# Layer-0 attention of a two-layer graph kernel: masked scores kept in PSUM, the softmax division given to GpSimd, and the steps of a turn in another order

## The chip, the cores and the metric

The kernel runs on one core of a Trainium2 chip. The metric is the device time of one execution in microseconds (us), the median of several.

## The reference

There are 64 independent graphs of 128 nodes with 256 features, and an adjacency matrix `adj` of zeros and ones for each. Two layers follow one another.

```python
# layer 0: 8 heads of 32, masked softmax, MLP of 1024
nx = LN(x) ; q, k, v = nx@wq+bq, nx@wk+bk, nx@wv+bv
scores = q@k.T / sqrt(32) + where(adj > 0, 0.1*adj*adj, -inf)
out = softmax(scores) @ v
x1 = x + out@wo + bo
x2 = x1 + gelu(LN(x1)@w1 + b1)@w2 + b2
# layer 1: one head of 256
w = softmax(where(adj == 0, -inf, (x2@Wq)@(x2@Wk).T / 16))
y = LN(x2 + (w @ (x2@Wv))@Wo + bo1) * gamma + beta
```

## The kernel before, in words

Each engine has its program written out by hand, and semaphores tie the five programs together. Work goes by groups: 4 graphs, 512 tokens, except for the first and the last group with 2 graphs each, which makes 17 groups. One turn of the kernel's loop works on four groups at once: `gp` (layer norm, queries, keys, values, scores and probabilities), `ga`, the group before it (attention output, `x1`, second layer norm), `gb`, the one before that (MLP and most of layer 1), and `gc` (the closing layer norm and the store). The turns for gp = 3 to 15 are alike (gp = 4 to 15 are a loop of 12); the turn of gp = 16 has half a group, and `first_turn` and `last_turn` are written apart. Every matrix product of the big layers is three TensorE matmuls (`mm3`, L395 to L400), of the high and low parts of both operands, so most copies out of PSUM come as a pair: ScalarE writes the high part, VectorE the low part (`low`, L1184). A wait for a low part is a wait for both.

The probabilities of layer 0 are worked on in pairs of graphs, q = 0 and 1, and within a pair in four parts r = 0 to 3, one PSUM bank each (banks 0 to 3). A part goes this way:

- `scores(gp, q)` on TensorE (L559) fills banks 0 to 3.
- `biased(g, q, r)` on VectorE (L1292, four instructions of 128x128, each with a read of the accumulator) subtracts the scores from the mask and writes the result to the SBUF tile `p_s`, with the row's extreme in `neg_max`.
- `exps` on ScalarE (L950, four of 128x128, each with an accumulator read) reads `p_s` and writes the exponentials back to the PSUM bank, sums in `psum`.
- `divided` on VectorE: the reciprocal of the sums (L1300), and a 128x512 multiplication out of the bank into `p_s` (L1302).
- `blocks` on VectorE (L1312) transposes 32x32 blocks of `p_s` into `pT`.
- SyncE stores `pT` to a DRAM scratch `parked` (4 DMAs per pair, L326) and loads it again in transposed order (L332), pair 0 into `pT` and pair 1 into `p_s`, for `attend` (L581) in the next turn.

`scores(gp, 1)` needs the banks back, and so waits for the last division of pair 0 (`dve_p`). Groups 0 and 1 use another way (a TensorE transpose) which the change leaves alone.

Other names used below: `h_low` (low part of the MLP's hidden tile; `mlp_up` number j reuses the bank of j - 4), `nxT_low` (its input for `project_k`), `residual2` (L1366, needed by `x2_transpose`, L664), `x2T_copy`, `x2T_high`, `x2T_low` (needed by `t_project`), `t_copy` (L1377, needed by `scores1`, L683), `biased1` (L1384) and `exps1` (L1014) of layer 1, and on GpSimd `rstd` (L1693, an inverse square root for a layer norm), `gain` and `offset` (L1773, L1778), `x_plus_bo`, `x1_plus_b2`, `x2_plus_bo` (L1752, L1762, L1768).

## Time and profile before

| what | us |
|---|---|
| median of 3 runs (lowest, highest) | 961.03 (959.05, 961.2) |
| the profiled execution, its own time | 959.66 |
| its span in the trace | 957.8 |
| TensorE busy in the span | 863.9 |
| VectorE busy | 725.0 |
| ScalarE busy | 618.6 |
| GpSimd busy | 387.9 |

The profiled execution is 1.4 us below the median and inside the range of the runs. Busy times are sums of the durations of an engine's instructions; matmuls overlap each other a little, so the distance from the start of one to the start of the next is the better measure of what TensorE does. The mean granted TensorE clock was 0.982 of full speed.

### The profile page before, as it was taken

To read this page: it belongs to the slowest core of one execution; us is meant where nothing else is said; L and a number is where in the kernel's file an instruction comes from. 1 tells how busy PE (TensorE), PEld (TensorE's weight loads), DVE (VectorE), ACT (ScalarE), POOL (GpSimd) and SP (SyncE) were. 2 spreads that over 40 slices of the span, in tenths; PEclk is the share of its full clock that TensorE was granted. 3 is DMA by queue.
4 is the path that set the end of the run, shared out by engine and by line. 5 is a ranking of instruction groups with operands and counts; after the bars stand their busy time and mean duration, and the time that the engine had idled before them with its cause. 6 is when DMAs were issued, how large, how long until landed. Compare 5 with 4: busy or idle time off the path is not lost.

```text
span 957.8 us, 21811 instructions
## 1 busy us (share of the span) xinstructions
PE 863.9 (90%) x7159; PEld 764.6 (80%) x7159; DVE 725.0 (76%) x2638; ACT 618.6 (65%) x1830; POOL 387.9 (41%) x258
## 2 busy tenths in 40 slices
PE   8987698989999898999999989998998989898996
PEld 7876488787878878788787878878787877888896
DVE  7686849599595968959597795959869595977645
ACT  6785666667576666757567565757756666684642
POOL 4534034525345452434535244453524445262412
PEclk9898799999999999999999999999999999999999
DMA  7100432524133242514324241342423224242000
GB/s 254 34 1 2 120 112 66 160 67 139 43 99 120 66 142 66 153 33 107 123 66 142 66 122 64 84 146 66 133 71 101 89 71 154 55 133 74 38 23 34
DMA packets 106304, 87.11 MB, mean 91 GB/s; under 512 B 3463, under 2 KB 91165, under 8 KB 106269
## 3 DMA queue, kind: packets, MB, share of 16 engines
q1 hardware_dynamic: 106252, 86.66, 29.9%
q8 instruction: 19, 0.31, 0.1%
q14 instruction: 17, 0.13, 0.0%
q10 hardware_dynamic: 16, 0.00, 0.0%
HBM read 47.85 MB, written 38.80 MB: 90 GB/s over the span
## 4 chain that ended last, share of the span: by engine, by line
PE 39%; DVE 35%; issue 15%; ACT 5%; POOL 3%; DVEq 1%; DMA 0%; POOLq 0%; SPq 0%; ACTq 0%
PE bank L398 10%; PE bank L400 9%; PE bank L399 9%; DVE p_s L1292 6%; DVE stats L1243 4%; DVE p_s L1302 4%; PE bank L581 3%; DVE nx L1260 3%; PE bank L714 3%; DVE nxT_lo L1184 2%; DVE x L1366 2%; PE bank L559 2%; DVE pT L1312 2%; POOL rstd L1693 2%; DVE x L1334 2%
## 5 line engine op out<-in xcount | busy, mean ns | idle before, releaser
L1292 DVE CUSTOM_DVE_ANT_0 p_s<-bank,bias 128x128 f32<-128x128 f32 x512 | 112.4, 284 | 140.7 <-PE bank L559 140.6
L950 ACT ACTIVATE bank<-p_s,neg_max 128x128 f32<-128x128 f32 x512 | 182.6, 357 | 44.5 <-DVE neg_max L1292 44.5
L398 PE MATMUL bank<-w_hi,hT_hi 128*128 128x256 f32 x512 | 146.2, 286 | 1.3 <-DVE hT_lo L1184 1.3
L400 PE MATMUL bank<-w_hi,hT_lo 128*128 128x256 f32 x512 | 144.2, 282 | 0.0
L399 PE MATMUL bank<-w_lo,hT_hi 128*128 128x256 f32 x512 | 144.0, 281 | 0.0
L1768 POOL TENSOR_TENSOR x<-x,bo_r 128x1024 f32<-128x1024 f32 (+1 forms) x16 | 37.3, 2333 | 234.0 <-PE bank L664 234.0
L398 PE MATMUL bank<-n2T_hi,w_hi 128*128 128x512 f32 (+1 forms) x272 | 111.2, 409 | 20.0 <-DVE hT_lo L1184 20.0
L1693 POOL TENSOR_TENSOR rstd<-ve,minus_half 128x4 f32<-128x4 f32 (+1 forms) x49 | 49.8, 1017 | 184.3 <-DVE ve L1253 184.1
L981 ACT ACTIVATE bank<-bank,vec_cols 128x512 f32<-128x512 f32 (+1 forms) x136 | 86.7, 637 | 33.4 <-PE bank L400 27.6
L400 PE MATMUL bank<-n2T_hi,w_lo 128*128 128x512 f32 (+1 forms) x272 | 105.1, 387 | 0.0
L399 PE MATMUL bank<-n2T_lo,w_hi 128*128 128x512 f32 (+1 forms) x272 | 105.0, 386 | 0.0
L398 PEld LDWEIGHTS bank<-w_hi,hT_hi 128*128 128x128 f32 x512 | 96.3, 188 | 4.5 <-DVE hT_lo L1184 2.2
L950 ACT ACTIVATION_READ_ACCUMULATOR bank<-p_s,neg_max 128x1 f32 x512 | 97.2, 190 | 0.0
L399 PEld LDWEIGHTS bank<-w_lo,hT_hi 128*128 128x128 f32 x512 | 96.4, 188 | 0.6
L400 PEld LDWEIGHTS bank<-w_hi,hT_lo 128*128 128x128 f32 x512 | 96.4, 188 | 0.0
L1302 DVE TENSOR_TENSOR p_s<-bank,rsum 128x512 f32<-128x512 f32 x128 | 88.5, 691 | 4.4
L1184 DVE TENSOR_TENSOR hT_lo<-bank,hT_hi 128x512 fp32r<-128x512 f32 (+1 forms) x136 | 85.2, 651 | 6.7 <-ACT hT_hi L893 6.7
L1312 DVE STREAM_TRANSPOSE pT<-p_s 128x512 f32<-128x512 f32 x116 | 82.1, 708 | 5.2 <-DMA parked<-pT 1.1
L893 ACT ACTIVATE hT_hi<-bank 128x512 fp32r<-128x512 f32 (+1 forms) x136 | 77.9, 573 | 5.3
L398 PEld LDWEIGHTS bank<-n2T_hi,w_hi 128*128 128x128 f32 x272 | 52.1, 192 | 35.9 <-DVE hT_lo L1184 26.1
L400 PEld LDWEIGHTS bank<-n2T_hi,w_lo 128*128 128x128 f32 x272 | 52.0, 191 | 10.9
L399 PEld LDWEIGHTS bank<-n2T_lo,w_hi 128*128 128x128 f32 x272 | 52.2, 192 | 9.3
(229 smaller groups left out, 2356.9 us busy)
## 6 DMA issues: line engine op xcount, KB each, us to landing
parked<-pT SPq DMA_DIRECT2D x116, 256.0 KB, 4.0
pT<-parked SPq DMA_DIRECT2D x15, 1024.0 KB, 5.5
p_s<-parked SPq DMA_DIRECT2D x14, 1024.0 KB, 7.7
xs<-in_x SPq DMA_DIRECT2D x15, 512.0 KB, 3.8
out<-y SPq DMA_DIRECT2D x14, 512.0 KB, 3.0
adj_i<-in_adj SPq DMA_DIRECT2D x15, 256.0 KB, 2.8
out<-y SPq DMA_DIRECT2D x3, 256.0 KB, 2.2
x2T_f<-in_L_gnn_w SPq DMA_DIRECT2D x1, 512.0 KB, 6.8
```

What stands on the lines that cost most here:

```text
L398: mm(out, a_hi, b_hi, start=first, stop=False)
L399: mm(out, a_hi, b_lo, start=False, stop=False)
L400: return mm(out, a_lo, b_hi, start=False, stop=last)
L893: return run(dst, src, ACT.Identity, **kw)
L950: last = run(bank[r][:, NODES * place:NODES * place + NODES], p_s[:, r, place, :], ACT.Exp, scale=-1.0, bias=neg_max[:, r, place:place + 1 ...
L981: run(h, h, ACT.Gelu, bias=cols["b1"][:, j:j + 1]).then_inc(act_h, 1)
L1184: return V.tensor_tensor(dst, src, hi.bitcast(f32), ALU.subtract)
L1243: V.bn_stats(ln_of(n, g)["stats"][:, b, :], src[:, b, :]).then_inc(ln_dve[n], 1)
L1292: last = V.tensor_tensor_reduce(p_s[:, r, place, :], bank[r][:, NODES * place:NODES * place + NODES], bias0[:, 2 * q + place // 2, :], -1. ...
L1302: V.tensor_tensor(p_s[:, r, :, :], bank[r][:, :].rearrange("p (h n) -> p h n", h=4), rsum[:, r, :, None].to_broadcast([128, 4, NODES]), AL ...
L1312: V.transpose(pT[:, r, :, :].rearrange("p b (l i) -> p l b i", l=4), p_s[:, r, :, :].rearrange("p l (b j) -> p l b j", j=32)).then_inc(dve ...
L1693: P.tensor_tensor(t["rstd"][:, 0:k], t["ve"][:, 0:k], minus_half[:, 0:k], ALU.pow).then_inc(ln_pool[n], 1)
```

## The change

The computation is the same. For the groups from 2 on, the masked scores are written back to their PSUM bank, ScalarE reads them there and writes the exponentials to `p_s`, VectorE does only the reciprocals (`inverse`), and GpSimd multiplies `p_s` by them in place (`normal`, 128x512 each, 8 in a turn), and `blocks` follows it. The banks are free for `scores(gp, 1)` once ScalarE has read them (`act_p`). In the turn, both attends and `scores(gp, 0)` come before all of `mlp_down`, `scores(gp, 1)` before its last quarter, `out_project(ga, 0)` before `x2_transpose`, `project_v(gp, 0)` before `t_project`, and `scores1` after the first half of `vo_project`, into bank 5 instead of 7. ScalarE, VectorE, GpSimd and SyncE are reordered to match; the diff shows TensorE's, ScalarE's and VectorE's turn whole.

```diff
@@ -197,7 +197,7 @@
         up_bank = (4, 5, 6, 7)
         usual_banks = dict(nx=(0, 1), k=(2, 3), q=(0, 1), v=(6, 7), av=(6, 7), wo=(6, 7), up=up_bank, down=(4, 5),
-                           n2=(4, 5), x2=(4, 5), t=(4, 5), s1=7, vo=(6, 7), p1=6, av1=(6, 7))
+                           n2=(4, 5), x2=(4, 5), t=(4, 5), s1=5, vo=(6, 7), p1=6, av1=(6, 7))
...
@@ -356,27 +357,29 @@
             load_adj(2)
             load_x(2)
+            load_adj(3)
             store_blocks(2, 0)
-            load_adj(3)
             load_x(3)
-
-            def turn(gp, ga, gc):
-                store_blocks(ga, 1)
-                load_blocks(ga, 0)
-                load_blocks(ga, 1)
+            store_blocks(2, 1)
+            for q in range(2):
+                load_blocks(2, q)
+
+            def turn(gp, gc):
                 if not is_last(gp):
...
                 if not is_last(gp):
                     load_x(gp + 1)
-
-            turn(3, 2, 0)
+                    store_blocks(gp, 1)
+                for q in pairs(gp):
+                    load_blocks(gp, q)
+
+            turn(3, 0)
             with sp.Fori(3, GROUPS - 3) as g:
-                turn(g + 1, g, g - 2)
-            turn(GROUPS - 2, GROUPS - 3, GROUPS - 5)
-            turn(GROUPS - 1, GROUPS - 2, GROUPS - 4)
-            load_blocks(GROUPS - 1, 0)
+                turn(g + 1, g - 2)
+            turn(GROUPS - 2, GROUPS - 5)
+            turn(GROUPS - 1, GROUPS - 4)
             store(GROUPS - 3)
@@ -488,7 +491,7 @@
                 pe.wait_ge(ln_dve[1], ln_end(g))
                 if not (isinstance(g, int) and g < 3):
-                    pe.wait_ge(dve_p, 4 * pair0(g))
+                    pe.wait_ge(act_p, 4 * pair0(g))
                 for t in range(KT):
@@ -544,7 +547,7 @@
                 if by_blocks(g):
                     if q == 1:
-                        pe.wait_ge(dve_p, 4 * pair0(g) + 4)
+                        pe.wait_ge(act_p, 4 * pair0(g) + 4)
                     elif isinstance(g, int) and g == 2:
@@ -571,6 +574,8 @@
                 if by_blocks(g):
                     pe.wait_ge(park_load[q], 16 * g - 16)
+                    if not is_last(g):
+                        pe.wait_ge(dve_h, HT * g - HT + 7 + q)
                 else:
@@ -596,8 +601,7 @@
                     pe.wait_ge(act_t, g)
                     pe.wait_ge(dve_t, g)
-                    if isinstance(g, int) and g == 1:
-                        pe.wait_ge(dve_s1, g)
+                    pe.wait_ge(dve_s1, g)
                 pe.wait_ge(ln_dve[2], ln_end(g))
...
@@ -673,9 +679,7 @@
                     last.then_inc(pe_t, 1)
-            def scores1(g, A):
-                if A:
-                    pe.wait_ge(dve_x1, pair0(g + 1) + size(g + 1) // 2)
+            def scores1(g):
                 pe.wait_ge(act_t, g + 1)
@@ -689,8 +693,8 @@
                 if P and q == 0:
                     pe.wait_ge(act_v, pair0(g + 2) + 1)
-                if q == 1:
-                    pe.wait_ge(dve_s1, g + 1)
+                if P and q == 1:
+                    pe.wait_ge(dve_x1, pair0(g + 1) + size(g + 1) // 2)
                 for b in (2 * q, 2 * q + 1):
@@ -734,21 +738,21 @@
                 project_q(gp, 0)
                 project_q(gp, 1)
-                mlp_down(gb, 0, (0,))
                 attend(ga, 0)
                 attend(ga, 1)
                 scores(gp, 0)
-                mlp_down(gb, 0, (1,))
-                mlp_down(gb, 1)
+                mlp_down(gb, 0)
+                mlp_down(gb, 1, (0,))
                 if size(gp) > 2:
                     scores(gp, 1)
+                mlp_down(gb, 1, (1,))
+                out_project(ga, 0)
                 x2_transpose(gb)
-                out_project(ga, 0)
                 out_project(ga, 1)
+                project_v(gp, 0)
                 t_project(gb)
-                project_v(gp, 0)
-                scores1(gb, True)
                 vo_project(gb, 0, True)
+                scores1(gb)
                 vo_project(gb, 1, True)
...
@@ -946,8 +950,15 @@
                 act.wait_ge(dve_s, 4 * (pair0(g) + q) + r + 1)
+                if by_blocks(g):
+                    if q == 1:
+                        act.wait_ge(dve_blocks, blocks_done(g, 0, r))
+                    elif r == 0:
+                        act.wait_ge(pe_av, pair0(g))
                 for place in range(4):
-                    last = run(bank[r][:, NODES * place:NODES * place + NODES], p_s[:, r, place, :], ACT.Exp, scale=-1.0,
+                    scored, part = bank[r][:, NODES * place:NODES * place + NODES], p_s[:, r, place, :]
+                    to, of = (part, scored) if by_blocks(g) else (scored, part)
+                    last = run(to, of, ACT.Exp, scale=-1.0,
                                bias=neg_max[:, r, place:place + 1], accum_out=psum[:, r, place:place + 1])
@@ -1037,24 +1048,21 @@
                 q_copy(gp, 1)
                 attn_high(ga, 0)
-                exps(gp, 0, 0)
-                exps(gp, 0, 1)
-                exps(gp, 0, 2)
-                exps(gp, 0, 3)
                 attn_high(ga, 1)
+                for r in range(HPT):
+                    exps(gp, 0, r)
+                if whole:
+                    exps(gp, 1, 0)
+                    exps(gp, 1, 1)
+                    exps(gp, 1, 2)
                 x2T_copy(gb)
                 x2T_high(gb)
                 if whole:
-                    exps(gp, 1, 0)
-                    exps(gp, 1, 1)
+                    exps(gp, 1, 3)
+                v_copy(gp, 0)
                 t_copy(gb)
-                if whole:
-                    exps(gp, 1, 2)
-                v_copy(gp, 0)
-                if whole:
-                    exps(gp, 1, 3)
+                vo_copy(gb)
                 exps1(gb)
-                vo_copy(gb)
                 n2T_copy(ga)
...
@@ -1284,26 +1294,29 @@
                 if q == 0 and r == 0:
                     dve.wait_ge(pool_bias, g + 1)
-                    dve.wait_ge(pe_av, pair0(g))
-                if q == 1 and by_blocks(g):
-                    dve.wait_ge(dve_blocks, blocks_done(g, 0, r))
+                    if not by_blocks(g):
+                        dve.wait_ge(pe_av, pair0(g))
                 dve.sem_inc(stand_dve, 1)
                 for place in range(4):
+                    scored = bank[r][:, NODES * place:NODES * place + NODES]
                     last = V.tensor_tensor_reduce(
-                        p_s[:, r, place, :], bank[r][:, NODES * place:NODES * place + NODES],
+                        scored if by_blocks(g) else p_s[:, r, place, :], scored,
                         bias0[:, 2 * q + place // 2, :], -1.0, -3.0 * MASKED, ALU.add, ALU.min, neg_max[:, r, place:place + 1])
                 last.then_inc(dve_s, 1)
+            def inverse(g, q, r):
+                dve.wait_ge(act_p, 4 * (pair0(g) + q) + r + 1)
+                V.reciprocal(rsum[:, r, :], psum[:, r, :]).then_inc(dve_r, 1)
+
             def divided(g, q, r):
                 count = 4 * (pair0(g) + q) + r + 1
-                dve.wait_ge(act_p, count)
-                V.reciprocal(rsum[:, r, :], psum[:, r, :]).then_inc(dve_r, 1)
+                inverse(g, q, r)
                 dve.wait_ge(dve_r, count)
...
             def blocks(g, q, r):
-                dve.wait_ge(dve_p, 4 * (pair0(g) + q) + r + 1)
+                dve.wait_ge(pool_p, blocks_done(g, q, r))
                 if r == 0:
@@ -1457,62 +1470,60 @@
                 moments(1, gp)
                 h_low(gb, 0)
+                norm1(gp)
+                for j in range(1, 5):
+                    h_low(gb, j)
                 sums3(gc)
-                norm1(gp)
-                h_low(gb, 1)
-                h_low(gb, 2)
+                nxT_low(gp)
                 moments(3, gc)
-                h_low(gb, 3)
+                h_low(gb, 5)
+                h_low(gb, 6)
+                h_low(gb, 7)
                 norm3(gc)
-                h_low(gb, 4)
-                nxT_low(gp)
-                for j in range(5, HT):
-                    h_low(gb, j)
+                attn_low(ga, 0)
+                attn_low(ga, 1)
                 for r in range(HPT):
                     biased(gp, 0, r)
-                attn_low(ga, 0)
-                divided(gp, 0, 0)
+                inverse(gp, 0, 0)
+                inverse(gp, 0, 1)
+                inverse(gp, 0, 2)
                 blocks(gp, 0, 0)
-                divided(gp, 0, 1)
+                inverse(gp, 0, 3)
+                residual2(gb, 0)
                 blocks(gp, 0, 1)
-                residual2(gb, 0)
-                divided(gp, 0, 2)
-                divided(gp, 0, 3)
-                attn_low(ga, 1)
                 blocks(gp, 0, 2)
-                residual2(gb, 1)
                 blocks(gp, 0, 3)
...
                     biased(gp, 1, 0)
                     biased(gp, 1, 1)
-                x2T_low(gb)
+                    biased(gp, 1, 2)
+                residual2(gb, 1)
+                if whole:
+                    biased(gp, 1, 3)
+                    inverse(gp, 1, 0)
+                    inverse(gp, 1, 1)
                 residual1(ga, 0, True)
                 if whole:
-                    biased(gp, 1, 2)
+                    inverse(gp, 1, 2)
+                    blocks(gp, 1, 0)
+                x2T_low(gb)
                 residual1(ga, 1, True)
                 if whole:
-                    biased(gp, 1, 3)
+                    inverse(gp, 1, 3)
+                    blocks(gp, 1, 1)
                 sums2(ga, 0)
                 sums2(ga, 1)
+                if whole:
+                    blocks(gp, 1, 2)
                 moments(2, ga)
                 t_copy(gb)
                 if whole:
-                    divided(gp, 1, 0)
-                    blocks(gp, 1, 0)
+                    blocks(gp, 1, 3)
                 norm2(ga)
                 biased1(gb)
-                if whole:
-                    divided(gp, 1, 1)
-                    blocks(gp, 1, 1)
                 vo_copy(gb)
-                if whole:
-                    divided(gp, 1, 2)
-                    blocks(gp, 1, 2)
                 n2T_low(ga)
                 inverse_sums1(gb)
-                if whole:
-                    divided(gp, 1, 3)
-                    blocks(gp, 1, 3)
                 residual3(gb, 0)
...
@@ -1777,21 +1792,44 @@
                 P.tensor_tensor(o[:, 0:graphs, :], o[:, 0:graphs, :], row_of("beta", graphs), ALU.add).then_inc(pool_out, 1)
+            def normal(g, q, r):
+                pool.wait_ge(dve_r, 4 * (pair0(g) + q) + r + 1)
+                P.tensor_tensor(p_s[:, r, :, :], p_s[:, r, :, :], rsum[:, r, :, None].to_broadcast([128, 4, NODES]),
+                                ALU.mult).then_inc(pool_p, 1)
+
...
             def turn(gp, ga, gb, gc):
                 rstd(1, gp)
                 pool.wait_ge(ln_dve[1], ln_end(gp))
-                if gc is not None:
-                    rstd(3, gc)
                 adjacency(gp)
                 edges(gp)
                 bias(gp)
-                if gc is not None:
-                    gain(gc, size(gc))
-                    offset(gc, size(gc))
-                x2_plus_bo(gb)
+                rstd(3, gc)
+                gain(gc, size(gc))
+                offset(gc, size(gc))
+                for q in pairs(gp):
+                    for r in range(HPT):
+                        normal(gp, q, r)
                 x_plus_bo(gp)
                 rstd(2, ga)
-                pool.wait_ge(ln_dve[2], ln_end(ga))
+                x2_plus_bo(gb)
                 x1_plus_b2(ga)
```

GpSimd, the turn of gp = 3 after the change, from the end of the mask's preparation on (`bias` is the mask of layer 0; `p_s<-p_s,rsum` is `normal`). Before, the rows with `p_s` are not there, and `x<-x,bo_r` stands ahead of `x_bo<-xs,bo_r`.

```order
L1741 TENSOR_TENSOR bias<-adj_s,adj_i 128x512
L1708 TENSOR_TENSOR rstd<-ve,minus_half 128x2
L1788 TENSOR_TENSOR y<-y,gamma_r 128x512
L1793 TENSOR_TENSOR y<-y,beta_r 128x512
L1797 TENSOR_TENSOR p_s<-p_s,rsum 128x512 x8
L1767 TENSOR_TENSOR x_bo<-xs,bo_r 128x1024
L1708 TENSOR_TENSOR rstd<-ve,minus_half 128x4
L1783 TENSOR_TENSOR x<-x,bo_r 128x1024
L1777 TENSOR_TENSOR x_b<-x,b_r 128x1024
L1749 TENSOR_SCALAR pen<-adj_f 128x512
```

So the second layer norm's `rstd` now stands behind eight multiplications and `x_plus_bo`.

ScalarE, the same turn, from the copies of the queries to the second layer norm's copies. Before (`bank,psum<-p_s` are the exponentials, four to a part):

```order
L938 ACTIVATE qT<-bank,vec_cols 128x512 x2
L893 ACTIVATE avT_hi<-bank 128x512
L950 ACTIVATE bank,psum<-p_s,neg_max 128x128 x16
L893 ACTIVATE n2T_hi<-bank 128x512
L893 ACTIVATE x2T_f<-bank 128x512 x2
L893 ACTIVATE x2T_hi<-x2T_f 128x512 x2
L950 ACTIVATE bank,psum<-p_s,neg_max 128x128 x8
L1007 ACTIVATE tT<-bank 128x512
L950 ACTIVATE bank,psum<-p_s,neg_max 128x128 x4
L893 ACTIVATE v<-bank 128x512
L950 ACTIVATE bank,psum<-p_s,neg_max 128x128 x4
L1014 ACTIVATE p,sum<-p,neg_max 128x128 x4
```

and after the change:

```order
L942 ACTIVATE qT<-bank,vec_cols 128x512 x2
L897 ACTIVATE avT_hi<-bank 128x512
L897 ACTIVATE n2T_hi<-bank 128x512
L961 ACTIVATE p_s,psum<-bank,neg_max 128x128 x28
L897 ACTIVATE x2T_f<-bank 128x512 x2
L897 ACTIVATE x2T_hi<-x2T_f 128x512 x2
L961 ACTIVATE p_s,psum<-bank,neg_max 128x128 x4
L897 ACTIVATE v<-bank 128x512
L1018 ACTIVATE tT<-bank 128x512
L1030 ACTIVATE vo<-bank 128x512
L1025 ACTIVATE p,sum<-p,neg_max 128x128 x4
```

Twelve exponentials (three parts of pair 1) now stand ahead of the copies of `x2T`, not behind them.

VectorE, the start of the same turn (layer norms and hidden tiles; `xs` is the new group, `y` the group that is closed). Before:

```order
L1184 TENSOR_TENSOR hT_lo<-bank,hT_hi 128x512
L1243 BN_STATS stats<-y 128x6 x2
L1260 TENSOR_SCALAR nx<-xs,mv,rstd 128x256 x4
L1184 TENSOR_TENSOR hT_lo<-bank,hT_hi 128x512 x2
L1250 BN_AGGR mv<-stats 128x2 x2
L1253 TENSOR_SCALAR ve<-mv 128x2
L1184 TENSOR_TENSOR hT_lo<-bank,hT_hi 128x512
L1260 TENSOR_SCALAR y<-y,mv,rstd 128x256 x2
L1184 TENSOR_TENSOR hT_lo<-bank,hT_hi 128x512
L1184 TENSOR_TENSOR nxT_lo<-bank,nxT_hi 128x512 x2
```

and after:

```order
L1194 TENSOR_TENSOR hT_lo<-bank,hT_hi 128x512
L1270 TENSOR_SCALAR nx<-xs,mv,rstd 128x256 x4
L1194 TENSOR_TENSOR hT_lo<-bank,hT_hi 128x512 x4
L1253 BN_STATS stats<-y 128x6 x2
L1194 TENSOR_TENSOR nxT_lo<-bank,nxT_hi 128x512 x2
L1260 BN_AGGR mv<-stats 128x2 x2
L1263 TENSOR_SCALAR ve<-mv 128x2
L1194 TENSOR_TENSOR hT_lo<-bank,hT_hi 128x512 x3
L1270 TENSOR_SCALAR y<-y,mv,rstd 128x256 x2
```

The closing norm of `y` no longer stands between the hidden tiles and `nxT_lo`.

## Rows read from the trace of the kernel before

**Rows 1.** Page, part 1: busy us, share of the span, instructions of each engine.
```profile
PE 863.9 (90%) x7159; PEld 764.6 (80%) x7159; DVE 725.0 (76%) x2638; ACT 618.6 (65%) x1830; POOL 387.9 (41%) x258
```
**Rows 2.** Timeline of GpSimd, one instruction of two turns: start, us, what, idle before.
```profile
210.14 2.40 POOL L1752 TENSOR_TENSOR x_bo<-xs,bo_r 128x1024 f32<-128x1024 f32 x1 [2.22 <-DVE x L1334]
...
831.23 2.40 POOL L1752 TENSOR_TENSOR x_bo<-xs,bo_r 128x1024 f32<-128x1024 f32 x1 [2.22 <-DVE x L1334]
```
**Rows 3.** Windows view of one turn: length, busy us, clock, DMA share, GB/s.
```profile
392.40:448.80 56.40, 51.68 (x435) 45.61 (x433) 44.22 (x163) 37.49 (x112) 24.31 (x15) 1.00 0.33 98
```
**Rows 4.** Timeline of TensorE in that turn: idle before and its releaser in brackets.
```profile
400.79 0.50 PE L398 MATMUL bank<-n2T_hi,w_hi 128*128 128x512 f32 x1 [1.10 <-DVE hT_lo L1184]
...
406.74 0.50 PE L398 MATMUL bank<-nxT_hi,wk_hi 128*128 128x512 f32 x1 [0.63 <-DVE nxT_lo L1184]
...
417.26 1.17 PE L559 MATMUL bank<-kT,qT 32*128 32x128 f32 x32
...
428.14 1.17 PE L559 MATMUL bank<-kT,qT 32*128 32x128 f32 x32 [0.97 <-DVE p_s L1302]
429.93 1.09 PE L664 MATMUL bank<-ident,x 128*128 128x128 f32 x8 [0.62 <-DVE x L1366]
...
439.21 2.02 PE L683 MATMUL bank<-x2T_f,tT 128*128 128x128 f32 x16 [1.19 <-DVE tT L1377]
```
**Rows 5.** Timeline of VectorE in that turn.
```profile
397.46 1.40 DVE L1243 BATCH_NORM_STATS2 stats<-y 128x6 f32<-128x256 f32 x4
398.77 1.36 DVE L1260 TENSOR_SCALAR nx<-xs,mv,rstd 128x256 f32<-128x256 f32 x4
...
403.06 1.83 DVE L1260 TENSOR_SCALAR y<-y,mv,rstd 128x256 f32<-128x256 f32 x4 [0.62 <-POOL rstd L1693]
...
405.41 1.27 DVE L1184 TENSOR_TENSOR nxT_lo<-bank,nxT_hi 128x512 fp32r<-128x512 f32 x2
...
418.74 0.29 DVE L1292 CUSTOM_DVE_ANT_0 p_s<-bank,bias 128x128 f32<-128x128 f32 x1 [10.26 <-PE bank L559]
...
422.13 0.68 DVE L1184 TENSOR_TENSOR avT_lo<-bank,avT_hi 128x512 fp32r<-128x512 f32 x1
```
**Rows 6.** Timeline of ScalarE: first exponential of pair 0, and what follows the sixteenth.
```profile
419.71 0.37 ACT L950 ACTIVATE bank<-p_s,neg_max 128x128 f32<-128x128 f32 x1 [2.51 <-DVE neg_max L1292]
...
425.90 0.58 ACT L893 ACTIVATE n2T_hi<-bank 128x512 fp32r<-128x512 f32 x1
```
**Rows 7.** Groups by line and form: count, busy us, mean ns, idle before.
```profile
L1302 DVE TENSOR_TENSOR p_s<-bank,rsum 128x512 f32<-128x512 f32 x128 | 88.5, 691 | 4.4
L1312 DVE STREAM_TRANSPOSE pT<-p_s 128x512 f32<-128x512 f32 x116 | 82.1, 708 | 5.2 <-DMA parked<-pT 1.1
...
L950 ACT ACTIVATE bank<-p_s,neg_max 128x128 f32<-128x128 f32 x512 | 182.6, 357 | 44.5 <-DVE neg_max L1292 44.5
L1014 ACT ACTIVATE p<-p,neg_max 128x128 f32<-128x128 f32 x62 | 24.2, 391 | 38.1 <-DVE neg_max L1384 38.1
...
L1752 POOL TENSOR_TENSOR x_bo<-xs,bo_r 128x1024 f32<-128x1024 f32 x15 | 36.0, 2399 | 38.3 <-DVE x L1334 37.4 <-DVE nx L1260 1.0
L1710 POOL TENSOR_SCALAR adj_i<-adj_g 128x512 f32<-128x512 f32 x15 | 30.7, 2050 | 3.0 <-POOL adj_g L1707 3.0
L1719 POOL TENSOR_TENSOR adj_s<-adj_s,adj_g 128x512 f32<-128x512 f32 x15 | 19.4, 1292 | 1.3
```
**Rows 8.** Timeline, SyncE's stores of a pair and the VectorE transpose held by them.
```profile
100.98 2.85 SPq L326 DMA_DIRECT2D parked<-pT  x4
...
107.33 0.71 DVE L1312 STREAM_TRANSPOSE pT<-p_s 128x512 f32<-128x512 f32 x1 [1.11 <-DMA parked<-pT]
```
**Rows 9.** Timeline of TensorE outside the like turns: gp = 3 and gp = 16.
```profile
115.30 0.80 PE L398 MATMUL bank<-n2T_hi,w_hi 128*128 128x512 f32 x1 [6.54 <-DVE hT_lo L1184]
...
876.85 0.87 PE L664 MATMUL bank<-ident,x 128*128 128x128 f32 x6 [2.70 <-DVE x L1366]
```

52 lines of the change are left out of this document (39 added, 13 removed).

## The prediction

> **What bounds the kernel now.** The page's first part comes first: TensorE is busy for 863.9 us of the span, VectorE for 725.0, GpSimd for 387.9 [rows 1]. Then the timeline, for how regular the work is: the same GpSimd instruction stands at 210.14 and, 11 turns on, at 831.23, so a turn of a whole group takes 56.46 us [rows 2]; 13 turns (gp = 3 to 15) make 734 of the span's 957.8 us. The windows view of one turn gives 51.68 us of TensorE in 56.40, and 44.22, 37.49 and 24.31 of VectorE, ScalarE and GpSimd, with the clock at full speed [rows 3]. So TensorE is the bound in each turn, and what can be won is its 4.72 us without work. The timeline says where they are [rows 4]: 1.10 for a hidden tile's low part, 0.63 for `nxT_lo`, 0.97 for the division of pair 0, 0.62 for `residual2`, 1.19 for `t_copy`, all of them waits for VectorE. From the start of the last matmul ahead to the start of the next, each costs 0.16 to 0.2 more than its bracket, since the matmuls overlap: I count 1.27, 0.79, 1.13, 0.80 and 1.35, and 0.47 of two small ones: 5.8 us in a turn. VectorE is not full, it is late: it has idle of 10.26 us elsewhere in the turn [rows 5].
>
> **The change, step by step, in one turn.** I write the old turn's times (it starts at 392.4) and walk the new order with the durations of the rows.
>
> Start of the turn. VectorE loses 8 multiplications of 691 ns [rows 7], 5.5 us a turn, four of them near the turn's end. `residual3` then waits for TensorE instead of for a division and ends 1.4 us sooner. The `y` statistics (1.40 at 397.46) no longer stand ahead of `nx` [rows 5]: `nx` ends at 398.1 instead of 400.1, the second hidden tile is at 398.7, TensorE wants it at 399.5. The 1.27 go. `y`'s norm (1.83 and 0.62 of waiting for GpSimd at 403.06) stood ahead of `nxT_lo` at 405.41 [rows 5]; with TensorE's transposes 1.3 sooner and only the statistics ahead, `nxT_lo` ends at 404.3, wanted at 404.7. The 0.79 go. GpSimd does the mask, `rstd`, `gain`, `offset` by 413.8, each duration as before.
>
> Pair 0. From scores to scores TensorE took 10.88 (417.26 to 428.14 [rows 4]): 1.1 of scores, three quarters of `mlp_down`, the stall of 1.13, so a quarter is 2.84 (with rounding; 2.88 by this). The scores come a quarter and the 2.06 earlier, at 412.3. From the start of the scores to the first masked one took 1.48 (417.26 to 418.74) and to the first exponential 2.45 (419.71) [rows 4 to 6]; sixteen exponentials took 6.19 (to 425.90), 1.55 a part [rows 6]. New: 414.75, and the banks are free at 420.95. TensorE has three quarters of `mlp_down` to do till 421.9: the 1.13 go. GpSimd's `normal` has no row. The nearest is a multiplication of two 128x512 SBUF tiles, 1292 ns (L1719); the bounds are 1.29 and 2.05 (L1710, as many elements) or 2.40 (L1752, twice as many, with a row spread over graphs as the reciprocals are spread over columns) [rows 7]. I take 1.29, the same operation and size. It is below the 1.55 of the exponentials, so GpSimd keeps up, the last `normal` ends at 422.6, and the last block (708 ns [rows 7]; 0.65 from start to start) at 423.75.
>
> Pair 1. Scores at 421.9, but `biased` is held behind that block: parts at 424.6, 425.45, 426.3, `residual2` at 426.95. TensorE's last quarter ends 425.8, `out_project` 427.2, so the 0.80 go. ScalarE has three parts till 429.35 and only then `x2T_copy`, `x2T_high` (2.05), so `x2T_low` ends at 432.2, and `t_project` wants it at 430.9 (from 429.93 to 439.21 [rows 4] are 9.28; without the stall of 1.35 and the 2.8 of `t_project` 5.1 are left, of `x2_transpose`, `out_project` and `project_v`, from 425.8 on). **A new wait, 1.3.** Close beside it runs a DMA: the store of pair 0 starts at 423.75, and the transpose of pair 1 may overwrite `pT` when it has landed. In [rows 8] that took 6.35 from the first issue (100.98 to 107.33): 430.1, then 0.65 of transposing, and `x2T_low` from 431.0: hidden by 0.2, and whatever exceeds it delays `x2T_low`.
>
> Layer 1. `vo_project` 0 covers part of `t_copy`, which VectorE reaches at 436.5 behind statistics and two blocks: `scores1` starts at 437.2, 0.7 late instead of 1.35. The second norm waits for `rstd`, behind the last `normal` (434.6), `x_plus_bo` (437.0) and itself (438.05). Its four instructions then run beside `x2_plus_bo` on GpSimd. Such an instruction took 0.32 to the next with GpSimd idle (`nx`, 1.36 for four) and 0.46 beside it (`y`, 1.83) [rows 5]: 439.9 instead of 439.4. The section Key points of the Trainium skill's page GPSIMD Engine Reference says that GpSimd shares SBUF interfaces with VectorE and contends with instructions in a 2-port mode or with two SBUF inputs; those two rows agree, and by it the divisions themselves, beside which VectorE reads PSUM or transposes, would cost VectorE nothing. `biased1` ends 440.8, `n2_transpose` is 0.5 late, `exps1` ends at 442.45 and `p1_transpose` is 0.75 late. From there to the end all is as before.
>
> Prices of no row: VectorE writing the masked scores to PSUM (none of its instructions does so now) and exponentials from PSUM to SBUF. For the second the bounds are 357 ns (SBUF to PSUM) and 391 (SBUF to SBUF) [rows 7]; I take the old spacing, 0.387. The Trainium skill's page ScalarE: Activation LUTs, Step-by-step: what each stage is for, calls PSUM the lower-latency destination for ScalarE. By 34 ns more on the twelve exponentials ahead of `x2T_copy` the turn's gain would be 0.4 smaller. For the first I take nothing; its bound is a doubling of the 0.21 spacing, which would make a part of VectorE's (0.85) 1.7, more than ScalarE's.
>
> **Sum.** Removed 5.8, added 1.3 + 0.7 + 0.5 + 0.75 = 3.2: 2.6 a turn, 34 over 13. Before turn gp = 3 the division and blocks of group 2 end some 5 us sooner, since `scores(2, 1)` is no longer behind them: of the 6.54 at 115.30 and the waits ahead of it I take 4.5. In turn gp = 16 the 2.70 at 876.85 goes (3, with the overlap) [rows 9]. Together 41. The profiled execution took 959.66, so 918; it was 1.4 below the median, so **919** against 961.03. Start-up, `last_turn` and DMA bytes don't change; the loads of `parked`, now issued at the end of a turn, land some 10 us ahead of `attend`.
>
> **The rivals.**
> (a) As above, 910 to 929: 0.60.
> (b) The new waits are longer. Candidates: the PSUM write, exponentials at 391, the store of pair 0 landing later than 6.35. Each us on the chain block, `biased`, exponentials, `x2T` is a us of the turn: with 0.5 to 1.8 more, 13 times, 926 to 943; taken as 929 to 945: 0.20. For it: the chain has 0.2 of slack. Against it: nothing in it was slower than its row.
> (c) Less wait than counted: if `t_copy`, `n2` and `p1` cover each other, up to 1.5 less per turn: 900 to 910: 0.11. The walk is pessimistic where VectorE could take things sooner.
> (d) Slower: `normal` is the new bound. Eight of them bring the second norm's `rstd`. With n us each, the chain is 8n - 12.95 later (pair 0: 4n - 6.35 over the block's time; pair 1 the same 4n, less 6.6 which the exponentials hide), and at n = 1.94 the 2.6 are gone. At 2.05 (L1710) a turn is 0.85 slower, 11 us over 13 of them, less the 7.5 of the two ends: 965. At 2.40 (L1752) 3.65 slower, 47 less 7.5: about 1000. For it: the reciprocals are spread along the innermost axis, which no row shows, and GpSimd needs 1.29 where VectorE needs 0.69 [rows 7]; the skill's GPSIMD page, Engine selection, gives two-input elementwise work to VectorE for this reason, and by it alone the time would rise. Against: L1719. 0.06.
> (e) The gaps close and open elsewhere in equal measure: 958 to 964, 0.03.
>
> **How the numbers follow.** The likeliest case gives 919. Leaving out (d), (e), half of (c) and a part of (b) leaves 2 in 10: 905 to 941. 0.3% is 2.9 us, about what a measurement of this kernel can tell from no change. Faster: (a), (b), (c), 0.91; the same: (e) and the part of (d) near its turning point, 0.05; slower: the rest of (d), 0.04.
>
> **What would show it.** Right: turns of 53.8 us by the spacing of `x_bo`; L1797 on GpSimd at 1.29; no wait of the second scores and of `x2_transpose`; none for `nxT_lo`; `t_project` waiting 1.3 for `x2T_lo`; short waits ahead of `scores1`, `n2` and `p1`; y's norm at 0.32 spacing. Wrong: L1797 above 1.55; VectorE's L1302 or ScalarE's L961 spaced wider than 0.21 and 0.39; a long wait of the transposes (L1325) for the store.

## The result, and the profile after

The changed kernel takes 983.88 us (median of 4 runs, 983.1 to 985.36) against 960.12 for the kernel before on the same chip (959.05 to 961.2): a ratio of 1.0249, 95% interval [1.0229, 1.0269]. It is 24 us slower, where 919 had been forecast. The profiled execution took 985.36 us, its span is 983.6, and the mean granted clock of TensorE fell from 0.982 to 0.947.

The page's first part, to be held against [rows 1], and the granted clock from its second:

```profile
PE 888.3 (90%) x7159; PEld 792.8 (81%) x7159; DVE 738.3 (75%) x2522; ACT 605.3 (62%) x1830; POOL 503.8 (51%) x374
## 2 busy tenths in 40 slices
...
PEclk8998799999989999998999989999999999989898
```

GpSimd has 116 us of work more, as the moved divisions should give. But VectorE, which lost 116 multiplications, is busier than before (738.3 against 725.0), and so is TensorE with the same 7159 matmuls. Something made existing instructions longer; on TensorE, as shown below, it was the clock. The groups by line and form say which (count, busy us, mean ns, idle before):

```profile
L1302 DVE CUSTOM_DVE_ANT_0 bank<-bank,bias 128x128 f32<-128x128 f32 x464 | 117.2, 326 | 2.3 <-PE bank L562 2.3
L1325 DVE STREAM_TRANSPOSE pT<-p_s 128x512 f32<-128x512 f32 x116 | 78.1, 694 | 9.1 <-DMA parked<-pT 7.6 <-POOL p_s L1797 1.2
L1270 DVE TENSOR_SCALAR nx<-x,mv,rstd 128x256 f32<-128x256 f32 x64 | 77.5, 1269 | 1.4 <-POOL rstd L1708 0.7
...
L1270 DVE TENSOR_SCALAR nx<-xs,mv,rstd 128x256 f32<-128x256 f32 x62 | 21.5, 408 | 8.3 <-POOL rstd L1708 7.7 <-issue 0.7
...
L961 ACT ACTIVATE p_s<-bank,neg_max 128x128 f32<-128x128 f32 x464 | 164.2, 404 | 88.2 <-DVE neg_max L1302 88.0 <-DVE pT L1325 0.2
...
L1797 POOL TENSOR_TENSOR p_s<-p_s,rsum 128x512 f32<-128x512 f32 x116 | 117.7, 1043 | 168.1 <-DVE rsum L1309 168.1
```

The two `nx` groups are the same instruction on tiles of the same shape: 408 ns in the first layer norm, 1269 in the second. The view of waits has the other end of it (engine, line, releaser, us in total, times, longest):

```profile
PEld bank L608 <- issue: 53.2, 15, 3.7
PE bank L608 <- DVE neg_max L1397: 50.3, 15, 3.5
```

L608 is `n2_transpose`, which reads `nx`; the page names `neg_max`, since `biased1` stands behind the norm on VectorE and is waited for too. One turn's timeline shows it. Here are GpSimd and VectorE:

```profile
618.52 2.40 POOL L1767 TENSOR_TENSOR x_bo<-xs,bo_r 128x1024 f32<-128x1024 f32 x1
...
619.28 0.69 DVE L1325 STREAM_TRANSPOSE pT<-p_s 128x512 f32<-128x512 f32 x1
...
620.26 0.68 DVE L1263 TENSOR_SCALAR ve<-mv 128x4 f32<-128x4 f32 x1
...
621.02 1.02 POOL L1708 TENSOR_TENSOR rstd<-ve,minus_half 128x4 f32<-128x4 f32 x1
622.01 2.36 POOL L1783 TENSOR_TENSOR x<-x,bo_r 128x1024 f32<-128x1024 f32 x1
...
622.20 2.33 DVE L1270 TENSOR_SCALAR nx<-x,mv,rstd 128x256 f32<-128x256 f32 x1
624.33 2.40 POOL L1777 TENSOR_TENSOR x_b<-x,b_r 128x1024 f32<-128x1024 f32 x1
624.45 2.44 DVE L1270 TENSOR_SCALAR nx<-x,mv,rstd 128x256 f32<-128x256 f32 x1
...
627.45 0.28 DVE L1397 CUSTOM_DVE_ANT_0 p<-bank,pen 128x128 f32<-128x128 f32 x1
```

And here is TensorE in the same turn, the instructions that waited:

```profile
616.69 0.50 PE L401 MATMUL bank<-x2T_hi,qk_hi 128*128 128x512 f32 x1 [0.46 <-DVE x2T_lo L1194]
...
621.68 2.02 PE L687 MATMUL bank<-x2T_f,tT 128*128 128x128 f32 x16 [0.51 <-DVE tT L1390]
...
628.62 1.09 PE L608 MATMUL bank<-ident,nx 128*128 128x128 f32 x8 [3.48 <-DVE neg_max L1397]
630.11 0.98 PE L711 MATMUL bank<-ident,p 128*128 128x128 f32 x4 [0.41 <-ACT p L1025]
```

The first `nx` starts 0.19 us after `x2_plus_bo` and ends 0.16 after its end; the second starts in that gap, 0.12 after `x1_plus_b2`, and ends 0.16 after that one. The last two take the usual 0.4 each. So one instruction of the norm is held by each addition, for as long as the addition lasts: 5.25 us from the first `nx` to `biased1` instead of some 1.3. Not every VectorE instruction is held. The transpose at 619.28 reads and writes SBUF and lies wholly beside the addition `x_plus_bo`, and it takes its usual 0.69. TensorE is idle for 3.48, and behind that its clock falls (windows view: length, busy us of PE, PEld, DVE, ACT, POOL, granted clock, DMA share, GB/s):

```profile
618.52:676.38 57.86, 53.00 (x434) 47.24 (x433) 45.47 (x155) 36.58 (x112) 32.22 (x24) 0.97 0.31 95
618.52:628.00 9.48, 6.10 (x46) 5.49 (x44) 9.40 (x20) 1.06 (x2) 8.11 (x5) 1.00 0.58 165
628.00:632.00 4.00, 2.98 (x18) 2.75 (x19) 2.35 (x8) 3.21 (x11) 2.55 (x2) 0.79 0.43 129
631.00:632.00 1.00, 1.00 (x7) 1.00 (x7) 0.94 (x3) 0.61 (x2) 0.30 (x1) 0.50 1.02 393
```

The 0.50 is 1.2 GHz, half the full 2.4. The fall is not at once: the first eight matmuls behind the idle still take 1.09 us at a clock of 1.00. Read in windows of 4 us, the clock falls to 0.79 or lower in each of the 13 like turns. In the turn of [rows 3] its mean was 1.00, and of the like turns of the kernel before only one shows a fall (0.84 and 0.73 from 484 to 492). GpSimd's timeline gives the length of a turn, 11 turns apart as in [rows 2]:

```profile
212.33 2.40 POOL L1767 TENSOR_TENSOR x_bo<-xs,bo_r 128x1024 f32<-128x1024 f32 x1
...
850.42 2.40 POOL L1767 TENSOR_TENSOR x_bo<-xs,bo_r 128x1024 f32<-128x1024 f32 x1
```

58.01 us, against 56.46 before. The 1.55 times 13 are 20 of the 24 us.

### The profile page after: what moved, and what is told of

Same layout as the page of the kernel before. It is cut to its first block, busy times and chain, and to the rows that moved or that the text cites. A ratio compares the mean times of both kernels' runs of the same rounds, so it can differ in the third digit from the quotient of the medians.

```text
span 983.6 us, 22014 instructions
## 1 busy us (share of the span) xinstructions
PE 888.3 (90%) x7159; PEld 792.8 (81%) x7159; DVE 738.3 (75%) x2522; ACT 605.3 (62%) x1830; POOL 503.8 (51%) x374
## 4 chain that ended last, share of the span: by engine, by line
PE 43%; DVE 19%; ACT 18%; issue 7%; POOL 1%; DVEq 0%; DMA 0%; SPq 0%; ACTq 0%; POOLq 0%
ACT p_s L961 13%; PE bank L401 11%; PE bank L402 11%; PE bank L403 11%; DVE nx L1270 7%; DVE pT L1325 3%; PE bank L718 3%; PE bank L586 3%; DVE bank L1302 2%; DVE stats L1253 2%; ACT p L1025 1%; ACT x2T_f L897 1%; PE bank L711 1%; PE bank L497 1%; DVE p L1397 1%
## 5 line engine op out<-in xcount | busy, mean ns | idle before, releaser
L961 ACT ACTIVATE p_s<-bank,neg_max 128x128 f32<-128x128 f32 x464 | 164.2, 404 | 88.2 <-DVE neg_max L1302 88.0
L1797 POOL TENSOR_TENSOR p_s<-p_s,rsum 128x512 f32<-128x512 f32 x116 | 117.7, 1043 | 168.1 <-DVE rsum L1309 168.1
L1302 DVE CUSTOM_DVE_ANT_0 bank<-bank,bias 128x128 f32<-128x128 f32 x464 | 117.2, 326 | 2.3 <-PE bank L562 2.3
L961 ACT ACTIVATION_READ_ACCUMULATOR p_s<-bank,neg_max 128x1 f32 x464 | 113.1, 244 | 0.0
L1325 DVE STREAM_TRANSPOSE pT<-p_s 128x512 f32<-128x512 f32 x116 | 78.1, 694 | 9.1 <-DMA parked<-pT 7.6
L1025 ACT ACTIVATE p<-p,neg_max 128x128 f32<-128x128 f32 x62 | 24.2, 391 | 94.0 <-DVE neg_max L1397 94.0
L1270 DVE TENSOR_SCALAR nx<-x,mv,rstd 128x256 f32<-128x256 f32 x64 | 77.5, 1269 | 1.4 <-POOL rstd L1708 0.7
L608 PE MATMUL bank<-ident,nx 128*128 128x128 f32 x128 | 23.0, 336 | 52.2 <-DVE neg_max L1397 50.3
```

The source lines that it names most:

```text
L961: last = run(to, of, ACT.Exp, scale=-1.0, bias=neg_max[:, r, place:place + 1], accum_out=psum[:, r, place:place + 1])
L1270: V.tensor_scalar(dst[:, b, :], src[:, b, :], t["mv"][:, b, 0:1], t["rstd"][:, b:b + 1], ALU.subtract, ALU.mult).then_inc(s, 1)
L1302: last = V.tensor_tensor_reduce(scored if by_blocks(g) else p_s[:, r, place, :], scored, bias0[:, 2 * q + place // 2, :], -1.0, -3.0 * MAS ...
L1325: V.transpose(pT[:, r, :, :].rearrange("p b (l i) -> p l b i", l=4), p_s[:, r, :, :].rearrange("p l (b j) -> p l b j", j=32)).then_inc(dve ...
L1797: P.tensor_tensor(p_s[:, r, :, :], p_s[:, r, :, :], rsum[:, r, :, None].to_broadcast([128, 4, NODES]), ALU.mult).then_inc(pool_p, 1)
```

## The experiments

Theory: VectorE's `tensor_scalar` is held by GpSimd's additions, which the change moved beside it; all else of the change gains about what was forecast. Rivals: the change gains little whatever happens to the norm; the loss is TensorE's clock, or any GpSimd work would do it.

**e1_norm_clear: GpSimd waits for the norm.**

```diff
                 rstd(2, ga)
+                pool.wait_ge(ln_dve[2], ln_end(ga))
                 x2_plus_bo(gb)
                 x1_plus_b2(ga)
```

> The changed kernel, with one wait put back on GpSimd: x2_plus_bo(gb) and x1_plus_b2(ga) start only when the second layer norm's four instructions on VectorE are done. Theory A (VectorE's tensor_scalar instructions are held while GpSimd adds two SBUF tiles; the idle of TensorE that this makes also lowers its clock): the four take 1.4 us instead of 5.3, a turn falls from 58.0 to about 53.5, the half-speed stretches in the turns go, and the kernel takes 910 to 930 us. Rival B (the second norm is late because rstd stands behind the divisions, or the exponentials are slower, and the held instructions cover a wait that is there anyway): 965 to 985.

Measured: 913.91 us (912.04 to 914.13), ratio to the kernel before 0.9508 [0.9482, 0.9535]. The norm is back at 409 ns. This kernel's timeline on GpSimd and VectorE:

```profile
580.73 1.02 POOL L1708 TENSOR_TENSOR rstd<-ve,minus_half 128x4 f32<-128x4 f32 x1
...
581.91 1.39 DVE L1270 TENSOR_SCALAR nx<-x,mv,rstd 128x256 f32<-128x256 f32 x4
...
583.47 2.38 POOL L1783 TENSOR_TENSOR x<-x,bo_r 128x1024 f32<-128x1024 f32 x1 [1.72 <-DVE nx L1270]
585.81 2.39 POOL L1777 TENSOR_TENSOR x_b<-x,b_r 128x1024 f32<-128x1024 f32 x1
```

And a turn of it in the windows view:

```profile
578.23:631.11 52.88, 51.52 (x434) 45.69 (x433) 41.80 (x155) 36.49 (x112) 32.27 (x24) 1.00 0.34 104
```

One wait on GpSimd, 1.72 us long, makes the kernel 70 us faster than the changed one. While those two additions run (583.47 to 588.2), VectorE does `biased1` at 0.21 spacing and the copy of `vo` in 0.69: these read PSUM and are not held.

**e2_one_add: the same wait one addition later**, so that only `x2_plus_bo` runs beside the norm.

```diff
                 x2_plus_bo(gb)
+                pool.wait_ge(ln_dve[2], ln_end(ga))
                 x1_plus_b2(ga)
```

> The changed kernel, with the wait put only ahead of x1_plus_b2(ga), so that x2_plus_bo(gb) alone still runs beside the second norm. Theory A: the norm is held for one GpSimd instruction, about 2.4 us, and takes 3.3 to 3.7 us; a turn of 55 to 56, 935 to 958 us. A theory in which VectorE only runs slower in proportion while GpSimd is busy, each instruction by some 0.14 us as beside the adjacency work before the change, gives a norm of 1.9 and under 925. Rival B: 965 to 985.

Measured: 935.34 us (934.14 to 937.02), ratio 0.9743 [0.9714, 0.9771], a turn of 54.4, which is below the 55 to 56 of theory A. Of the four instructions one is held, three are not (durations min/median/max in the view of the tile `nx`):

```profile
L1270 DVE TENSOR_SCALAR nx<-x,mv,rstd x4: 402/403/2328, 592.7 to 595.6; 128x256 f32<-128x256 f32 x4
```

So the first addition costs 21 us of the kernel, the second 49: the first is partly hidden, since TensorE still has the end of `vo_project` to do, and behind the second the clock falls as well. In e2 TensorE is idle for 1.45 us at this place instead of 3.48, and the clock falls in two turns only.

**e3_old_collide: the kernel before, with its wait for the norm left out**, so that `x1_plus_b2` runs beside the norm in the old order too.

```diff
                 rstd(2, ga)
-                pool.wait_ge(ln_dve[2], ln_end(ga))
                 x1_plus_b2(ga)
```

> The kernel before the change, with one wait taken away on GpSimd: x1_plus_b2(ga) no longer waits for the second norm (it reads x1 as the norm does, and writes another tile). Theory A: the norm's four instructions at 440.65 are held until about 442.2, biased1 and the second half of vo_project are 1.5 us later, 13 times: 975 to 990 us. Rival B: within 3 us of the kernel before.

Measured: 980.8 us (977.95 to 982.81), ratio 1.0214 [1.0178, 1.0251]; the group `nx<-x` has a mean of 666 ns (402 before), most turns are 57.5 us, and three, in which the clock falls too, 58.1 to 58.2. The hold needs nothing of the change but the place of an addition. Nor is a shared tile the condition: `x1_plus_b2` reads the tile that the norm reads, the `x2_plus_bo` of e2 works on another one, and both hold it.

**e4_divide_dve: e1 with the division on VectorE**, ahead of each transpose, none on GpSimd.

```diff
             def blocks(g, q, r):
-                dve.wait_ge(pool_p, blocks_done(g, q, r))
+                dve.wait_ge(dve_r, 4 * (pair0(g) + q) + r + 1)
+                V.tensor_tensor(p_s[:, r, :, :], p_s[:, r, :, :], rsum[:, r, :, None].to_broadcast([128, 4, NODES]),
+                                ALU.mult).then_inc(dve_p, 1)
+                dve.wait_ge(dve_p, 4 * (pair0(g) + q) + r + 1)
...
-                for q in pairs(gp):
-                    for r in range(HPT):
-                        normal(gp, q, r)
```

> As e1_norm_clear, but the division stays on VectorE (a 128x512 multiplication of p_s by the reciprocals just ahead of each block's transpose), GpSimd does none. It measures what giving the division to GpSimd is worth in the new order. Theory A, with VectorE's chain the limit: 5.5 us a turn more of VectorE, of which 1.5 to 2.5 lie on the chain to x2T_low: 20 to 35 us slower than e1_norm_clear. If the order alone brings the gain: within 5 us of it.

Measured: 956.85 us (956.0 to 959.5), ratio 0.9963 [0.995, 0.9977], a turn of 56.0. The division's place is worth 43 us, more than the 20 to 35 expected. The new order with the masked scores in PSUM, which e4 keeps, is worth only some 4. VectorE's multiplication, whose two inputs are in SBUF, also stretches GpSimd's `x_plus_bo` beside it from 2.40 to 2.90 us.

**e5_copy_add: e2 with `x2_plus_bo` reduced to one tensor input.** The addition of `bo1` is left out.

```diff
-                P.tensor_tensor(x[:, 0:k, :], x[:, 0:k, :], row_of("bo1", k), ALU.add).then_inc(pool_x2b, 1)
+                P.tensor_scalar(x[:, 0:k, :], x[:, 0:k, :], 0.0, None, ALU.add).then_inc(pool_x2b, 1)
```

> The arrangement of e2_one_add, in which x2_plus_bo alone runs beside the four nx instructions of the second norm; here it is written as an instruction with one tensor input (x2 plus the constant 0.0, the same 128x1024 tile; the addition of bo1 is left out). Theory, VectorE's tensor_scalar is held by GpSimd's instruction with two tensor inputs: nx comes down from 825 ns to 400 to 550, the turn to 52.9 to 53.5, the time to 914 to 923 us. Rival, any GpSimd instruction of that length holds it: nx stays near 825 ns, the turn at 54.4, the time at 933 to 938 us.

Measured: 925.04 us (923.83 to 925.93), ratio 0.9649 [0.9633, 0.9665], between both expectations. `nx` has a mean of 705 ns. GpSimd's instruction first, then the first and the last `nx` of that turn:

```profile
586.96 2.79 POOL L1784 TENSOR_SCALAR x<-x 128x1024 f32<-128x1024 f32 x1
...
587.13 1.01 DVE L1270 TENSOR_SCALAR nx<-x,mv,rstd 128x256 f32<-128x256 f32 x1
...
588.71 1.18 DVE L1270 TENSOR_SCALAR nx<-x,mv,rstd 128x256 f32<-128x256 f32 x1
```

With two tensor inputs the first `nx` was held for 2.33; with one, four of them fit into 2.8 us, the first and the last stretched to 1.01 and 1.18. "Only two-input instructions hold it" falls; so does "all alike". The instruction is also another operation (`tensor_scalar` for `tensor_tensor`); whether the inputs or the operation make the difference was not tried. Beside the norm the one-input instruction costs 11 us of e1's time, the addition 21.

**e6_filler: matmuls against the clock.** 14 products of `ident` by itself stand on TensorE ahead of its wait for the norm; their result is overwritten.

```diff
                     pe.wait_ge(dve_s1, g)
+                    for i in range(14):
+                        mm(bank[4][:, 0:128], ident[:, :], ident[:, :], start=True, stop=True)
                 pe.wait_ge(ln_dve[2], ln_end(g))
```

> The changed kernel, with 14 matmuls ident by ident of 128 columns (their result is overwritten) on TensorE ahead of its wait for the second norm, in the turns where that wait stands at 3.48 us. The norm is as late as before, only TensorE is not idle meanwhile. Theory, a part of the 21 us that the change lost is the clock at half speed behind the idle (106.1 us of it against 36.3): the half-speed stretches in the turns go, with some 5 us a turn at twice the spacing 2 to 2.5 us come back in each of 13, 950 to 958 us. Rival, the clock costs nothing since VectorE sets the pace there: 980 to 988 us. If the filler itself delays the transposes, up to 4 us more than either.

Measured: 1027.24 us (1022.31 to 1029.85), ratio 1.0721 [1.0699, 1.0742]: outside both. I had put them behind the wait for `biased1`, which itself ends after the norm, so they filled nothing. TensorE's timeline:

```profile
585.75 5.99 PE L606 MATMUL bank<-ident 128*128 128x128 f32 x28 [3.39 <-DVE neg_max L1399]
591.57 1.04 PE L610 MATMUL bank<-ident,nx 128*128 128x128 f32 x8
```

They run at half speed (5.8 us from start to start, granted clock 0.53; e9 has 3.3 at 1.00), and the products behind them at full.

**e9_filler_early: the same 14 products ahead of the wait for `biased1`.**

```diff
                     pe.wait_ge(dve_t, g)
+                    for i in range(14):
+                        mm(bank[4][:, 0:128], ident[:, :], ident[:, :], start=True, stop=True)
                     pe.wait_ge(dve_s1, g)
```

> As e6_filler, the changed kernel with 14 matmuls of ident by ident, but ahead of the wait for biased1 (and so for the second norm, which stands before it on VectorE) and not behind it; in e6_filler they began only after the idle of 3.4 us, took 5.8 us at half speed, and the products behind them were at full speed again. Theory, the clock costs 2.3 us of each turn (the 5.8 us of the filler less the 3.4 to 3.5 by which e6_filler's turn is longer): with the filler in the idle, the clock stays up and the time is 984 less 13 times 2.3, 950 to 958 us. Rival, the clock's fall has little to do with the loss: 978 to 988 us.

Measured: 960.8 us (959.83 to 962.41), ratio 1.0001 [0.9988, 1.0015]: 3 us above the theory's range, 17 below the rival's. The norm is as late as in the changed kernel, and the clock does not fall. The timeline of VectorE and TensorE:

```profile
609.74 5.34 DVE L1272 TENSOR_SCALAR nx<-x,mv,rstd 128x256 f32<-128x256 f32 x4
...
612.51 3.29 PE L605 MATMUL bank<-ident 128*128 128x128 f32 x28
616.05 1.09 PE L610 MATMUL bank<-ident,nx 128*128 128x128 f32 x8 [0.26 <-DVE neg_max L1399]
```

The turn in the windows view:

```profile
606.05:662.47 56.42, 54.70 (x462) 48.88 (x461) 45.56 (x155) 36.44 (x112) 32.21 (x25) 1.00 0.32 98
```

Work that computes nothing makes the changed kernel 23 us faster: that is the clock's part, 1.6 us a turn, less than the 2.3 I read out of e6 (whose filler also hid the wait of 0.4 to 0.5 for `p`). Of the 70 us between the changed kernel and e1, 23 are the clock and 47 the lateness itself.

**e7_t_copy: e1, with `t_copy` ahead of `moments(2)` on VectorE.**

```diff
+                t_copy(gb)
                 moments(2, ga)
-                t_copy(gb)
```

> e1_norm_clear with t_copy ahead of moments(2) on VectorE. Theory, the 0.51 us that TensorE waits for tT and the 0.41 for p are behind VectorE's aggregation and a 0.68 us tensor_scalar beside x_plus_bo: tT comes 0.9 us sooner, scores1 waits for nothing, the turn is 52.3 to 52.5, the time 906 to 909 us. Rival, the second norm, now 0.3 to 0.6 later, takes it back: 912 to 915 us.

Measured: 907.67 us (907.45 to 908.87), ratio 0.9464 [0.9448, 0.948], a turn of 52.53. The theory's time holds; the wait for `tT` is gone, but the one for `p` is still 0.40, and one of 0.36 has come ahead of `n2_transpose`. `ve<-mv` is back at 0.17 us: it now starts only 0.05 before the end of `x_plus_bo`.

**e8_old_order: the kernel before, in its old order of TensorE and ScalarE, with the new parts alone.** VectorE has `inverse` where `divided` stood, its blocks come some places later, `residual2` of the first pair comes ahead of the second block, and GpSimd's turn, for all groups with a `gc`, is this:

```diff
+                for r in range(HPT):
+                    normal(gp, 0, r)
+                if gc is not None:
+                    x2_plus_bo(gb)
+                    x_plus_bo(gp)
+                    rstd(2, ga)
+                    pool.wait_ge(ln_dve[2], ln_end(ga))
+                if size(gp) > 2:
+                    for r in range(HPT):
+                        normal(gp, 1, r)
                 x1_plus_b2(ga)
```

> The kernel before in its old order, with the new parts alone: masked scores to PSUM, exponentials to the probability tile, VectorE's reciprocals, GpSimd's multiplications (pair 0 behind offset, pair 1 behind its wait for the second norm). With e4_divide_dve (new order, old division, 957) it tells whether order and division are worth something apart. Theory, VectorE's 5.5 us a turn are worth as much in either order: the second scores' wait and most of t_copy's go, 925 to 940 us. Rival, the division pays only in the new order: 950 to 965 us.

Measured: 923.66 us (919.33 to 924.31), ratio 0.9617 [0.9589, 0.9644]. This is 1.3 us below the theory's range. In the old order the division on GpSimd, together with the masked scores in PSUM and the banks that come free sooner, is worth 36 us; no run parts the three there. In the new order the division's place alone is worth 43 (e1 against e4). With the division on GpSimd, the new order gives 10 us more than the old (e1 against e8), if GpSimd waits.

**e10_best: e8 with three moves on VectorE.**

```diff
+                t_copy(gb)
                 sums2(ga, 0)
...
-                t_copy(gb)
...
-                norm2(ga)
                 biased1(gb)
+                norm2(ga)
...
-                norm3(gc)
                 h_low(gb, 4)
                 nxT_low(gp)
+                norm3(gc)
```

> e8_old_order (old order of TensorE and ScalarE, new parts) with three moves on VectorE: t_copy ahead of sums2, biased1 ahead of norm2, norm3 behind nxT_low. Theory, TensorE's two waits in its turn of 53.55 us, 1.41 for tT and 0.63 for nxT_lo, go and nothing new comes: a turn of 51.6 to 52.0, 899 to 905 us, below e7_t_copy (907.7). Rival, one of the moved steps is late for the next product (the second norm for its transposes, or the exponentials of layer 1): half of it comes back, 908 to 916 us.

Measured: 907.76 us (905.83 to 909.07), ratio 0.9446 [0.9428, 0.9465], a turn of 52.45. That is above the theory's 899 to 905 and just below the rival's 908 to 916. Both old waits are gone, and one has come that neither named: a block waits for GpSimd, `vo_copy` is behind it, and TensorE behind that. The timeline of the two:

```profile
578.49 0.71 DVE L1323 STREAM_TRANSPOSE pT<-p_s 128x512 f32<-128x512 f32 x1 [1.25 <-POOL p_s L1795]
579.12 0.65 DVE L1401 COPY vo<-bank 128x512 f32<-128x512 f32 x1
...
579.83 0.38 PE L399 MATMUL bank<-wv_hi,nxT_hi 128*128 128x256 f32 x1 [0.92 <-DVE vo L1401]
```

**e11_vo_first: e10 with `vo_copy` ahead of that block.**

```diff
+                vo_copy(gb)
                 if whole:
                     inverse(gp, 1, 2)
                     blocks(gp, 1, 0)
-                vo_copy(gb)
```

> e10_best with vo_copy ahead of the first block of pair 1 on VectorE. In e10_best that block waits 1.25 us for GpSimd's multiplication, vo_copy stands behind it, and TensorE's next product waits 0.92 for vo_copy. Theory, these 0.92 go and nothing follows them: a turn of 51.5 us, 894 to 898 us. Rival, the blocks, then later, delay the store of pair 1 and the attends or the low part of n2T behind them: 904 to 910 us.

Measured: 906.23 us (903.6 to 907.29), ratio 0.9425 [0.9403, 0.9447]: the theory misses, the rival's figure holds, its reason does not. The 0.92 are gone, and TensorE waits instead for a hidden tile of the next MLP. VectorE comes to that tile no later than in e10: 18.94 us after `x_bo` starts, against 18.99. It is TensorE that is there sooner, so here VectorE sets the pace. TensorE's timeline:

```profile
591.90 0.50 PE L399 MATMUL bank<-n2T_hi,w_hi 128*128 128x512 f32 x1 [1.25 <-DVE hT_lo L1192]
```

e7, e10 and e11 end within 2 us of each other, so I name none of them the best. They are 52 to 54 us faster than the kernel before.

## Why the prediction was wrong

**The step that failed is the second norm.** The prediction said of its four instructions beside `x2_plus_bo`: "0.46 beside it (`y`, 1.83) [rows 5]: 439.9 instead of 439.4". The row was real, but what ran on GpSimd beside it was not an addition of two tiles. In the trace of before, GpSimd's timeline had these at that time:

```profile
402.87 0.61 POOL L1707 CAST adj_g<-adj_i 128x512 f32<-128x512 int32 x1
403.67 2.07 POOL L1710 TENSOR_SCALAR adj_i<-adj_g 128x512 f32<-128x512 f32 x1 [0.20 <-POOL adj_g L1707]
```

Both have one tensor input. As e5 shows, such an instruction stretches the norm but lets all four parts through (2.76 us beside one of 2.79), while one with two holds a part until its own end (e2). And I priced one addition where two follow each other, so the hold came twice: 5.25 us from start to `biased1` instead of 1.85. In the kernel before the wait `ln_dve[2]` kept `x1_plus_b2` away from the norm, and `x2_plus_bo` stood ahead of `rstd`; the diff removed the first and moved the second. I read that wait as order only, and e3 shows that it was worth 20 us.

The Trainium skill's page SBUF — State Buffer, section SBUF: two separate sides, says more than the page I quoted: the port pair that VectorE and GpSimd share is an exclusive lock, held for the whole instruction, and not shared bandwidth. For the additions the trace agrees: 2.33 and 2.44 us of `nx` beside 2.36 and 2.40 of addition. For e5's one-input instruction it does not: four `nx` fit into its 2.79 us.

**A second step was missing:** that a wait can cost clock. I put every late us at one us. After the 3.48 us of idle the clock fell to half, which e9 measures at 23 us. The rows could not price it: the turn of [rows 3] was at full clock.

Without those two, e1 is the kernel that the prediction described: 913.9 against 919. That the two are so close is in part luck, since the turns gained 12 us more than forecast and the ends nothing of their 7.5. (The sum as it stands, 33.8 and 7.5 off 959.66 and 1.4 on, gives 919.7.) Its steps:

- Start of the turn: right. The waits for the hidden tile and for `nxT_lo` are gone; `y`'s norm takes 1.37 with GpSimd idle, as said.
- `normal`: 1043 ns where 1.29 was taken, below the lower bound. Rival (d), that it becomes the bound, never came near.
- Exponentials out of PSUM: spaced 0.343 us (599.96 to 604.76 for 14 steps in the changed kernel), not 0.387. It is the source that counts: those of layer 1, from SBUF to SBUF, are 0.39 apart. Sixteen take 0.7 us less; a mis-sized term in the kernel's favour. Their durations of 404 ns overlap, so that the mean alone would have misled.
- Masked scores into PSUM: spaced 0.25 instead of 0.21, no doubling, and hidden behind the exponentials but for the first part (the first exponential comes 1.13 us behind the first masked score, not 0.97).
- The second scores and `x2_transpose` wait for nothing: right. `t_project`'s new wait was to be 1.3: it is 0.46. The store of pair 0 did use up its slack of 0.2 and holds the transpose by 0.24 us.
- `scores1`: 0.51 measured, 0.7 said; `p1`: 0.41, 0.75 said; `n2` without the hold: none, 0.5 said.
- The turn: 52.9 in e1, 53.8 said. Against 56.46 that is 46 over 13 turns, and the whole gain is 46 between the profiled executions (914.0 against 959.66): the 7.5 us that I counted outside the like turns came to nothing. At gp = 3 the wait of 6.54 [rows 9] is now this, in TensorE's timeline of the changed kernel:

```profile
105.67 0.79 PE L401 MATMUL bank<-n2T_hi,w_hi 128*128 128x512 f32 x1 [3.27 <-DVE y L1420]
...
116.33 0.79 PE L401 MATMUL bank<-n2T_hi,w_hi 128*128 128x512 f32 x1 [5.17 <-DVE hT_lo L1194]
```

It became 1.4 us shorter, a wait of 3.27 stands ahead of it, and the place in the program comes 1.0 us later than before (116.33 against 115.30), of which 0.9 are there already at a `scores` of 58.09 us (57.23 before). So the first turns gained nothing. What holds them was not tried.
